# One ring of 60 row slots for the gathered k and v rows, products written over k, and a pad row for unused slots

## The reference

```python
q = (x @ Wq + bq).reshape(n, H, C)
k = (x @ Wk + bk).reshape(n, H, C)
v = (x @ Wv + bv).reshape(n, H, C)
attn = einsum('nhc,mhc->hnm', q, k) / sqrt(C)
neg = where(adj == 0, -inf, attn)
e = where(adj == 0, 0, exp(neg - max(neg)))
alpha = e / sum(e)
out = einsum('hnm,mhc->nhc', alpha, v)            # n x (H*C)
x_r = x @ Ws + bs
beta = sigmoid(concat([out, x_r, out - x_r]) @ Wb)
return layernorm(x + beta * x_r + (1 - beta) * out)
```

## Time and profile before

| | |
|---|---|
| median of 3 runs | 2084.48 us |
| the profiled execution | 2082.6 us, its span 2080.8 us |
| busy of the span | TensorE 57%, VectorE 67%, GpSimd 58%, ScalarE 37% |
| TensorE's granted clock | 0.668 |
| GpSimd: gathers (L464) | 1057, 1064.3 us |
| VectorE: product L684, reduction L687, weighing L707 | 152.7, 152.6, 152.6 us |
| DMA | 431.9 MB, of it 291.3 on SP's queue and 129.9 on GpSimd's |

### The profile page before, as it was taken

How to read it: one execution, slowest core, us unless ns; L and a number is a source line. 1 busy time by engine, 2 the same in 40 slices (tenths; PEclk the granted TensorE clock), 3 DMA queues, 4 the chain that set the end, 5 groups by cost and what they waited for, 6 DMA issues and landing times. The chain is left out here.

```text
span 2080.8 us, 19706 instructions
## 1 busy us (share of the span) xinstructions
PE 1188.8 (57%) x4601; PEld 748.1 (36%) x4601; DVE 1392.1 (67%) x3885; ACT 760.3 (37%) x1290; POOL 1201.6 (58%) x1342
## 2 busy tenths in 40 slices
PE   6334454655455455555456455545544353799998
PEld 5113233332233233233223233222233242256887
DVE  5878888887688678878868877877874566121010
ACT  3243233445246234634454454554411001222313
POOL 2347767776777777777767747747676773000000
PEclk9656667666677667668777767767765565655555
DMA  9757666768677677788688868858522232500000
GB/s 369 275 220 265 217 230 250 261 217 294 249 276 265 232 283 281 262 292 305 219 294 307 294 234 289 304 191 304 198 85 80 83 91 99 183 1 0 0 1 2
DMA packets 127968, 431.86 MB, mean 208 GB/s; under 512 B 29310, under 2 KB 62683, under 8 KB 94827
## 3 DMA queue, kind: packets, MB, share of 16 engines
q1 hardware_dynamic: 63194, 291.25, 37.1%
q0 software_dynamic: 55728, 129.92, 19.5%
q10 hardware_dynamic: 8928, 9.44, 1.3%
HBM read 430.75 MB, written 19.31 MB: 216 GB/s over the span
## 5 line engine op out<-in xcount | busy, mean ns | idle before, releaser
L464 POOL DMA_INDIRECT s_kv<-kv_rows,s_rec_in x1057 | 1064.3, 1007 | 402.3 <-issue 329.8
L494 PE MATMUL s_ps_w<-s_mask,s_bit_w 128*128 128x512 bf16 x1008 | 371.0, 513 | 496.9 <-ACT s_mask L576 496.2
L560 PE MATMUL s_acc<-s_kv,ident 128*128 128x128 f32 x2114 | 368.1, 354 | 257.6 <-DVE s_kv L707 257.6
L576 ACT ACTIVATE s_mask<-s_adj_in 128x2048 bf16<-128x2048 f32 x252 | 477.5, 1896 | 48.6 <-PE s_ps_w L494 29.4
L560 PEld LDWEIGHTS s_acc<-s_kv,ident 128*128 128x128 f32 x2114 | 353.5, 265 | 311.0 <-DVE s_kv L707 309.9
L494 PEld LDWEIGHTS s_ps_w<-s_mask,s_bit_w 128*128 128x128 bf16 x1008 | 101.1, 116 | 728.4 <-ACT s_mask L576 612.1
L684 DVE TENSOR_TENSOR s_prod<-s_kv,s_ps_q 128x1792 f32<-128x1792 f32 (+17 forms) x76 | 152.7, 2009 | 121.4 <-DMA s_kv<-kv_rows,s_rec_in 119.9
L609 ACT ACTIVATE s_ps_q<-s_sc 128x56 f32<-128x56 f32 (+17 forms) x76 | 16.8, 221 | 482.6 <-DVE s_sc L698 482.6
L707 DVE TENSOR_TENSOR s_kv<-s_kv,s_ps_q 128x1792 f32<-128x1792 f32 (+17 forms) x76 | 152.6, 2007 | 29.5 <-ACT s_ps_q L609 25.4
L687 DVE TENSOR_REDUCE s_raw<-s_prod 128x56 f32<-128x1792 f32 (+17 forms) x76 | 152.6, 2007 | 6.0 <-issue 0.4
L1166 DVE CUSTOM_DVE_ANT_0 d_sc<-d_ps_s,d_pen 128x1024 f32<-128x1024 f32 x32 | 39.2, 1225 | 165.9 <-PE d_ps_s L1087 165.9
(11 more groups left out here) (195 smaller groups left out, 1465.9 us busy)
## 6 DMA issues: line engine op xcount, KB each, us to landing
s_adj_in<-in_adj SPq DMA_DIRECT2D x247, 1024.0 KB, 7.2
s_kv<-kv_rows,s_rec_in POOLq DMA_INDIRECT x1057
kv_rows<-s_kv SPq DMA_DIRECT2D x16, 512.0 KB, 9.4
s_rec_in<-node_records SPq DMA_DIRECT2D x62, 106.0 KB, 7.6
s_adj_in<-in_adj ACTq DMA_DIRECT2D x5, 1024.0 KB, 19.8
s_kv<-in_x_cols SPq DMA_DIRECT2D x4, 1024.0 KB, 8.4
d_kT<-in_x_cols SPq DMA_DIRECT2D x1, 4096.0 KB, 12.2
d_adj<-in_adj SPq DMA_DIRECT2D x1, 4096.0 KB, 19.8
```

Source lines behind the costliest of these rows:

```text
L464: nc.gpsimd.indirect_dma_start(out=kv[:, k % RING, s], out_offset=None, in_=kv_dram[:, :], in_offset=bass.IndirectOffsetOnAxis(ap=rec_in_u ...
L494: last = nc.tensor.matmul(w[:], bit_w[:, SLABS - 1 - slab], mask[:, k % 2, s * WORD:(s + 1) * WORD], start=False, stop=(slab == SLABS - 1))
L560: last = nc.tensor.matmul(acc[:, c * D:(c + 1) * D], ident[:], kv[:, k % RING, s, D:2 * D], start=(s == 0), stop=(s == SIZES[k] - 1))
L576: nc.scalar.activation(mask[:, q % 2], adj_in[:, q % ADJ_RING], ACT.Sign, accum_out=edges[:, t, h:h + 1]).then_inc(masked, 1)
```

## The change

One ring of 60 slots replaces the three buffers. `ring_plan` lays the units out one behind the other, goes back to slot 0 where one would not fit, and notes for each unit how many units must be summed before its gathers (`FREE`); at most 12 are in flight, each with a semaphore of its own in turn. The products go over the gathered k in `kv`; `prod` is gone. Row 0 of `kv_rows` is a pad row of ones, node rows stand one further down, and an unused slot holds 0 and fetches the pad row. So that unused entries come out as 0, the bit order of the slabs and the position code are reversed, and with them the order of the list. The stages of the start are 7 in place of 8, since the memory of `kv` is smaller.

```diff
-RING = 3
+KV_SLOTS = 60
+FLIGHT = 12
+O_RING = 3
-STAGES = 8
+STAGES = 7
...
+def ring_plan():
+    starts, free, pos = [], [], 0
+    for k, s in enumerate(SIZES):
+        if pos + s > KV_SLOTS:
+            pos = 0
+        last = [j for j in range(k) if starts[j] < pos + s and pos < starts[j] + SIZES[j]]
+        starts.append(pos)
+        free.append(max([j + 1 for j in last] + [k + 1 - FLIGHT]))
+        pos += s
+    return starts, free
+
+
+START, FREE = ring_plan()
...
 def slots_landed(k):
-    return 16 * sum(s for j, s in enumerate(SIZES[:k + 1]) if j % RING == k % RING)
+    return 16 * sum(s for j, s in enumerate(SIZES[:k + 1]) if j % FLIGHT == k % FLIGHT)
+
+
+def stores_of(b):
+    return 16 * sum(g % STAGES == b for g in range(GROUPS))
...
-        kv_dram = nc.dram_tensor("kv_rows", (N, 2 * D), F32, kind="Internal").ap()
+        kv_dram = nc.dram_tensor("kv_rows", (1 + N, 2 * D), F32, kind="Internal").ap()
...
-        kv = sb("kv", [P, RING, MAX_S, 2 * D], F32)
-        prod = sb("prod", [P, MAX_S * D], F32)
+        kv = sb("kv", [P, KV_SLOTS, 2 * D], F32)
...
-        kv_stage = x_stage[:, 8192:16384].rearrange("p (a j c) -> p a j c", a=STAGES, j=GROUP)
+        kv_stage = x_stage[:, 8192:8192 + STAGES * GROUP * 2 * D].rearrange("p (a j c) -> p a j c", a=STAGES, j=GROUP)
...
+            sp.wait_ge(consts, 2)
+            for k in range(2):
+                sp.dma_start(kv_dram[0:1, k * D:(k + 1) * D], ones[:]).then_inc(pad_stored, 16)
             q = ADJ_RING
             for g in range(GROUPS):
-                row = g * GROUP * P
+                row = 1 + g * GROUP * P
...
-            nc.gpsimd.memset(x_stage[:, 16384:], 0.0).then_inc(consts, 1)
+            nc.gpsimd.memset(slot_last[:, 1:2], float(SLOTS[1])).then_inc(consts, 1)
...
             for b in range(STAGES):
-                pool.wait_ge(kv_stored[b], 16 * (GROUPS // STAGES))
+                pool.wait_ge(kv_stored[b], stores_of(b))
+            pool.wait_ge(pad_stored, 16 * 2)
...
-                need(pool, summed, k + 1 - RING)
+                need(pool, summed, FREE[k])
                 for s in range(SIZES[k]):
                     col = LIST_AT + first_slot(p, c) + s
                     nc.gpsimd.indirect_dma_start(
-                        out=kv[:, k % RING, s], out_offset=None, in_=kv_dram[:, :],
+                        out=kv[:, START[k] + s], out_offset=None, in_=kv_dram[:, :],
                         in_offset=bass.IndirectOffsetOnAxis(ap=rec_in_u[:, p % RECS, col:col + 1], axis=0),
-                        bounds_check=last_node, oob_is_err=False).then_inc(gathered[k % RING], 16)
+                        bounds_check=last_row, oob_is_err=False).then_inc(gathered[k % FLIGHT], 16)
...
-                    last = nc.tensor.matmul(w[:], bit_w[:, SLABS - 1 - slab], mask[:, k % 2, s * WORD:(s + 1) * WORD],
+                    last = nc.tensor.matmul(w[:], bit_w[:, slab], mask[:, k % 2, s * WORD:(s + 1) * WORD],
...
-                dve.wait_ge(gathered[b], slots_landed(k))
-                part = prod[:, 0:s * D].rearrange("p (s c) -> p s c", c=D)
-                nc.vector.tensor_tensor(part, kv[:, b, 0:s, 0:D],
-                                        ps_q[r][:, 0:D].unsqueeze(1).to_broadcast([P, s, D]), ALU.mult)
-                dve.drain()
-                nc.vector.tensor_reduce(raw[:, 0:s * H], part.rearrange("p s (h c) -> p (s h) c", h=H), AX, ALU.add)
+                dve.wait_ge(gathered[k % FLIGHT], slots_landed(k))
+                part = kv[:, b:b + s, 0:D]
+                nc.vector.tensor_tensor(part, part, ps_q[r][:, 0:D].unsqueeze(1).to_broadcast([P, s, D]), ALU.mult)
+                dve.drain()
+                nc.vector.tensor_reduce(raw[:, 0:s * H].rearrange("p (s h) -> p s h", h=H), part.rearrange("p s (h c) -> p s h c", h=H), AX, ALU.add)
...
-                    nc.vector.memset(slot[:, LIST_AT + m:LIST_AT + width], float(N))
-                last = nc.vector.tensor_scalar(slot[:, LIST_AT:LIST_AT + m], top[:, 0:m], -1.0, float(BASE + N - 1),
-                                               ALU.mult, ALU.add)
+                    nc.vector.memset(slot[:, LIST_AT + m:LIST_AT + width], 0.0)
+                last = nc.vector.tensor_scalar(slot[:, LIST_AT:LIST_AT + m], top[:, 0:m], float(BASE - 1),
+                                               float(BASE - 1), ALU.max, ALU.subtract)
```

More of the change, by code:

```diff
@@ L197, in sparse_tiles @@
         xs = sb("xs", [P, 2, P], F32)
-        o_r = sb("or", [P, RING, 2 * D], F32)
+        o_r = sb("or", [P, O_RING, 2 * D], F32)
         raw = sb("raw", [P, MAX_S * H], F32)
@@ L243, in sparse_tiles @@
         slot_last = sb("slot_last", [P, T], F32)
-        earlier = prod[:, 0:T * (WINDOW - 1)].rearrange("p (t k) -> p t k", k=WINDOW - 1)
+        earlier = words[:, 0:T * (WINDOW - 1)].rearrange("p (t k) -> p t k", k=WINDOW - 1)
         slots_of = sb("slots_of", [P, T], F32)
@@ L274, in sparse_tiles @@
         kv_ready = sem("kv_ready")
+        pad_stored = sem("pad_stored")
         kv_stored = [sem(f"kv_stored{i}") for i in range(STAGES)]
@@ L287, in sparse_tiles @@
         rec_loaded = [sem(f"rec_loaded{i}") for i in range(RECS)]
-        gathered = [sem(f"gathered{i}") for i in range(RING)]
+        gathered = [sem(f"gathered{i}") for i in range(FLIGHT)]
         rows_turned = sem("rows_turned")
@@ L307, in sparse_tiles @@
         over_summed = sem("over_summed")
-        x_stage = kv[:].rearrange("p a s c -> p (a s c)")
+        x_stage = kv[:].rearrange("p s c -> p (s c)")
         xT = x_stage[:, 0:N]
-        kv_stage = x_stage[:, 8192:16384].rearrange("p (a j c) -> p a j c", a=STAGES, j=GROUP)
+        kv_stage = x_stage[:, 8192:8192 + STAGES * GROUP * 2 * D].rearrange("p (a j c) -> p a j c", a=STAGES, j=GROUP)
         rec_u = rec[:].bitcast(U32)
@@ L314, in sparse_tiles @@
         steps = [(tiles, k, SLOTS[tiles[k]] - SLOTS[tiles[k + 1]]) for tiles in WINDOWS for k in range(len(tiles) - 1)]
-        POOL_CONSTS = 24 + len(steps) + len(WINDOWS) + (T - 1) + (WINDOW - 1)
+        POOL_CONSTS = 23 + len(steps) + len(WINDOWS) + (T - 1) + (WINDOW - 1)
         def need(eng, sem, value):
@@ L397, in _ @@
             pool.wait_ge(consts, 6)
-            nc.gpsimd.iota(words[64:65, :], pattern=[[0, 2], [-1, WORD // 2]], base=WORD // 2 - 1, channel_multiplier=0,
+            nc.gpsimd.iota(words[64:65, :], pattern=[[0, 2], [1, WORD // 2]], base=0, channel_multiplier=0,
                            allow_small_or_imprecise_dtypes=True).then_inc(consts, 1)
@@ L422, in _ @@
                 nc.gpsimd.memset(listed[:, t:t + 1], float(8 * list_rounds(t))).then_inc(consts, 1)
-            nc.gpsimd.memset(slot_last[:, 1:2], float(SLOTS[1])).then_inc(consts, 1)
             for tiles in WINDOWS:
@@ L432, in _ @@
             last_node = pool.to_reg(N - 1)
+            last_row = pool.to_reg(N)
             def scatter_records(w):
@@ L559, in _ @@
                 for s in range(SIZES[k]):
-                    last = nc.tensor.matmul(acc[:, c * D:(c + 1) * D], ident[:], kv[:, k % RING, s, D:2 * D],
+                    last = nc.tensor.matmul(acc[:, c * D:(c + 1) * D], ident[:], kv[:, START[k] + s, D:2 * D],
                                             start=(s == 0), stop=(s == SIZES[k] - 1))
@@ L603, in copy_r @@
                 act.wait_ge(q_ready, p)
-                nc.scalar.copy(o_r[:, p % RING, D:2 * D], ps_q[p % 2][:, D:2 * D]).then_inc(r_copied, 1)
+                nc.scalar.copy(o_r[:, p % O_RING, D:2 * D], ps_q[p % 2][:, D:2 * D]).then_inc(r_copied, 1)
             def exp_chunk(k):
@@ L675, in score_chunk @@
                 p, c = UNITS[k]
-                r, b, s = p % 2, k % RING, SIZES[k]
+                r, b, s = p % 2, START[k], SIZES[k]
                 if c == 0:
@@ L702, in weigh_chunk @@
                 p, c = UNITS[k]
-                r, b, s = p % 2, k % RING, SIZES[k]
+                r, b, s = p % 2, START[k], SIZES[k]
                 dve.wait_ge(expd, k + 1)
-                v = kv[:, b, 0:s, D:2 * D].rearrange("p s (h c) -> p s h c", h=H)
+                v = kv[:, b:b + s, D:2 * D].rearrange("p s (h c) -> p s h c", h=H)
                 e_sh = e[r][:, 0:s * H].rearrange("p (s h) -> p s h", h=H)
@@ L807, in attend @@
             def attend(p):
-                r, o, n = p % 2, p % RING, n_chunks(p)
+                r, o, n = p % 2, p % O_RING, n_chunks(p)
                 sums, total = acc[:, 0:D], dens[:, r, 0]
@@ L860, in _ @@
             nc.vector.memset(place[0:1, :], -float(1 << 24))
-            nc.vector.memset(place[32:33, 0:WORD // 2], float(WORD // 2))
+            nc.vector.memset(place[32:33, WORD // 2:], float(WORD // 2))
             nc.vector.tensor_copy(place[64:65, :], words[64:65, :]).then_inc(places_ready, 1)
@@ L1121, in _ @@
             act.wait_ge(adj_loaded, 16)
-            act.dma_start(v_rows[:], kv_dram[:, D:2 * D].rearrange("(b p) c -> p b c", p=P)).then_inc(v_in, 16)
```

(1 more changed line is left out.)

2 lines of the change are left out of this document (1 added, 1 removed).

## The result

The changed kernel takes 2114.89 us (median of 4 runs, 2112.29 to 2116.18) against 2084.70 us for the kernel before on the same chip: 1.0143 times as long, 95% interval 1.013 to 1.0155, or 30.2 us more. The profiled execution took 2116.18 us, its span 2114.4. Slower was forecast, but by 8.7 us: the time lies outside the range that was given.

A forecast was written before the change was run, and what follows sets the result against it. VectorE and GpSimd were taken to bound the sparse half by turns, handing over by dependence. 8.6 + 1.0 - 0.9 = +8.7 us on 2084.5 gave 2093.2; range 2081 to 2106, the forecast's own 2088.7 to 2104.

The forecast's parts named there:

- The ring, early: Units 4, 6 and 7 wait for the sum of the unit two before; unit 7's multiply comes 8.6 us late.
- The bound up to 15.4: Early delay at unit 7 if units 4 and 7 land 5.3 us after their last gather, not 1.9: 15.4 us.
- Carried to the end: The early delay of 8.6 us passes through `spot` and every later handover to the end; chance 0.60.
- The rival in which it is absorbed: The early stall is taken up by gaps but for 1 to 3 us: 2084 to 2087; chance 0.18.
- The ring, later: Waits at units 22, 23, 37 cost nothing; from unit 41 more units in flight, gaining 0.9 us at unit 60.
- Products over k: Multiply into kv's strided k half and strided reduction cost at most 2 ns x 76 more: nothing.
- The pad row: Unused slots' fetches add 19.5 MB; GpSimd pays nothing, about six handovers pay 0 to 0.4 us each: 1.0 us.
- The rival of the hot pad row: Pad gathers in each window's first tile land slower than GpSimd issues them: 30 to 90 us, 2115 to 2180; chance 0.09.
- Seven stages: At the start, groups 7 to 10 wait for stores 0 to 3: nothing, up to 1 us if stores are late.
- The faster rival: Adj loads go earlier, so late landings before units 31, 39, 47, 55 fall to 1.9 us: 13.6 gained, 2074; chance 0.13.
- The sum: Whole kernel: early ring 8.6, pads 1.0, late ring gain 0.9 taken off: +8.7 us, giving 2093.2.
- The upper end of the forecast's own range: Whole kernel with the early stall carried at 15.4 us and pads at 2.5: 2104 us.

The follow-up runs named there:

- The kernels with later scatters: Scatters of windows 3 to 8 issued two units later: kernel before 2054.51 us; with 128 pads: 84 slots, 8 stages 2043.09, three buffers, 7 stages 2056.95.

## Why the prediction was right, and where it was wrong

- *The ring, early*: right in place and mechanism, short in size. Units 4 and 6 waited for the unit two before (11.48 and 6.30 us), the four scatters no longer waited for `spot`, and unit 7 came behind them. Taken was 8.6 us, and 0.9 off for the late gain; measured, with that gain in it, it costs 12.5 alone on the kernel before (2096.9 against 2084.4) and 10.5 in the changed kernel (10.4 with 128 pads). The term that was mis-sized is the landing. 1.9 us was taken since unit 7 had had it before, with 5.3 as the other bound; unit 7's rows now landed after 5.2 us (ring alone) and 5.0 us (128 pads), while units 4 and 6 of the ring-alone kernel landed after 1.8 and 1.2. The bound up to 15.4 held it. The landing isn't a property of a unit: the same unit 7 landed after 1.9 us in some kernels and 5 in others. What else was on the queues at the new time may be the reason; that wasn't tried.
- *Carried to the end*: right. With the ring alone the delay is 14.2 us at unit 7, 13.5 at unit 15, 13.3 at unit 36, 12.6 at unit 60 and 12.0 at unit 75. The rival in which it is absorbed fell.
- *The ring, later*: right, but for 1.5 us before unit 22 in the changed kernel. No ring wait stands before unit 60, and the gain is lost in the wait for `spot`. The kernels with later scatters bear that out: 84 slots in place of three buffers, with the same pads, gave 13.9 us there (2057.0 to 2043.1) and 2.8 us without them (2088.0 to 2085.1).
- *Products over k*: right, nothing, 2008 and 2007 ns.
- *The pad row*: this step failed, the 1.0 us that the sum has for it. The bytes were right (149.48 MB). GpSimd paid nothing, which was right too (1007 ns). But the price was an average over gathers of scattered rows, 3.12 us per MB, and so 0.4 us for a gather of all pads, 1.0 us in the sum. Gathers whose entries nearly all go to one row cost far more: unit 6's 20 gathers took 45.1 us to land, where they took 26.9 without fetches, of which 25.7 are issue. With 128 pad rows the queue took 453 us of each engine in place of the 406 of before, so there 19.56 MB of pads cost 2.4 us per MB, less than the price taken; with one row it was 6.4. By the Trainium skill, "DMA: Bandwidth & Descriptors", section "Anatomy of one DMA — SWDGE (gpsimd) path", such a DMA takes 2.0 us plus bytes/436e3. By that, the bytes of a gather take an estimated 0.3 us and can't fall behind an issue every 1.30 us. With 128 pad rows the trace agrees so far that 20 gathers landed 2.2 us after those without fetches (29.1 against 26.9 us); with one row it doesn't, at 2.3 us per gather (45.1 over 20). 128 pad rows in place of the one gave 16.5 us back, and the cost showed only at handovers, as the step had reasoned: by the multiplies, the kernel with one row is behind that with 128 by 7 us at unit 3, 20 at unit 6, 12 at unit 7, 17 at unit 15, 20 at unit 18, 22 at unit 36 and 18 at unit 75.
- *The rival of the hot pad row* was the right one, at a chance of 0.09, and its sign was named in advance (gathers with many pads land later than others). It was priced too high (30 to 90 us, against 16.5): it let nine gathers of pads fall behind at each of six places, while much of each place's lateness was absorbed, as the list of the step above shows. No gather before came near 128 reads of one row. The prediction's "27 at most" holds for unit 0; by the drawn adjacency, ranked, unit 4's first gather has 40. Either way no row of the trace bounded this cost; the range should have taken it in as an unknown cost, from 0 up to where the gathers' landing becomes the pace.
- *The rest*: fetching pads as such, and what isn't told apart from it, is 3.6 us against 1.0. *Seven stages*: right, nothing.
- *The faster rival*, adj transfers no longer colliding: nothing of it was seen in the kernels with the early scatters. The late landings before units 31, 39, 47 and 55 were to fall to 1.9 us; with the ring alone they were 3.4, 4.5, 5.1 and 5.9 (3.3, 4.5, 5.0 and 5.3 before). The rival also has gathers and adj loads share queues; by the profile they are on two, GpSimd's and SP's. The ring of 84 without early waits was 1.001 of before (1.0001 to 1.0019), not faster.
- *The sum*: taken 8.6 + 1.0 - 0.9; measured 10.4 for the ring (with its late gain in it), 16.5 for one row in place of many, 3.6 for the rest. With four pad rows the change takes 2093.0 us, which is 9.4 over before: the sum without its missing term was nearly right, but in part by luck, since fetching pads cost more than taken, and unit 7 landed there after the 1.9 us that the sum had, which it didn't with 128 pads or with the ring alone. The upper end of the forecast's own range, 2104, doesn't follow from its terms: 2084.5 + 15.4 + 2.5 is 2102.4, and 2101.5 with the gain of 0.9.

## What to carry over

A padding index is a real address: when most of the 128 nodes fetch the same DRAM row, landing is no longer covered by the average price per byte. So give the pad several rows (with four, 9.4 us of the 30.2 were left here), and count the most reads of one row in the indices before trusting an average. A ring that shares slots is judged by the stretch with the largest units, not by the mean depth, and a deeper one pays only once the wait that stands behind buffers is moved: 84 slots in place of three buffers gave 2.8 us before the scatters were moved and 13.9 after.

## What the hardware showed that was not expected

- Twenty gathers, 2042 of whose 2560 rows are one and the same 1 KB row, landed in 45.1 us: 2.3 us each, about 45 KB/us of pads (2042 KB in 45.1 us), while GpSimd issues one in 1.30 us. Eighteen with 1944 of 2304 took 40.6 us and 40.4 us in two kernels. Two neighbouring rows in halves: 37.4 us; four: 30.5; 128: 29.1. The queue's time per engine over the whole run goes the same way: 531 us with one row, 477 with two (22.8% of 2093.9), 462 with four (22.1% of 2090.5), 453 with 128 (21.6% of 2096.8), 402 with none (19.2% of 2093.0, the ring alone).
- The time from a unit's last gather to its use was 1.9 us with four pad rows and 5.0 with 128 for the same unit 7, whose gathers began at the same time (299.30 and 299.32). The cause is open.
